# One list schedule for another: the same attention kernel with new tables of places

## The reference

```python
q = hidden_state @ Wq + bq                      # 512 x 1024
k = encoder_hidden_state @ Wk + bk              # 512 x 256
v = encoder_hidden_state @ Wv + bv              # 512 x 256
scores = einsum('bkgld,bksd->bkgls', q, k) / sqrt(32) + mask
attn = softmax(scores, axis=-1)
out = einsum('bkgls,bksd->bkgld', attn, v)
out = out @ Wo + bo
x = out + hidden_state
return (x - mean) * rsqrt(var + 1e-6) * gamma + beta
```

## Time and profile before

| | us |
|---|---|
| three timed runs | 1784.44, 1790.49, 1792.52 |
| their median | 1790.49 |
| profiled execution | 1783.61 |
| its span, first to last instruction | 1781.6 |
| mean granted TensorE clock | 0.967 |

### The profile page before, as it was taken

How to read it: one execution, slowest core, us unless ns; L and a number is a source line. 1 busy time by engine, 2 the same in 40 slices (tenths; PEclk the granted TensorE clock), 3 DMA queues, 4 the chain that set the end, 5 groups by cost and what they waited for, 6 DMA issues and landing times.

```text
span 1781.6 us, 38449 instructions
## 1 busy us (share of the span) xinstructions
PE 1638.9 (92%) x14048; PEld 1102.8 (62%) x14048; DVE 1469.6 (82%) x2773; ACT 1352.6 (76%) x3186; POOL 936.7 (53%) x731
## 2 busy tenths in 40 slices
PE   3898889899999989999899999999999998999895
PEld 2565556576667666677566666666665765657653
DVE  4589888789888897889889898888977988877875
ACT  3568777668887797877878789877987778786783
POOL 5426342426843476534845268444765348455381
PEclk8999999999999999999999999999999999999998
DMA  9659887747875578665896478856796647954321
GB/s 177 185 142 217 240 238 192 172 122 181 282 215 136 138 218 271 170 151 142 217 286 168 118 187 276 219 132 146 200 280 177 151 125 210 292 163 112 94 99 54
DMA packets 357291, 325.00 MB, mean 182 GB/s; under 512 B 145776, under 2 KB 248176, under 8 KB 357104
## 3 DMA queue, kind: packets, MB, share of 16 engines
q1 hardware_dynamic: 357104, 322.56, 67.9%
HBM read 244.85 MB, written 83.89 MB: 185 GB/s over the span
## 4 chain that ended last, share of the span: by engine, by line
PE 64%; DVE 19%; ACT 7%; issue 4%; SPq 4%; DMA 1%; POOL 0%; DVEq 0%; ACTq 0%
PE bank L1958 34%; PE bank L2041 15%; PE bank L2021 9%; DVE turned_p L1856 9%; DVE bank L1843 7%; ACT probs L1748 4%; PE bank L2056 2%; SPq L1516 2%; PE bank L1998 1%; PE bank L2081 1%; PE bank L2069 1%; DVE shift L1843 1%; SPq L1464 1%; ACT part L1731 1%; DVE x_t L1816 1%
## 5 line engine op out<-in xcount | busy, mean ns | idle before, releaser
L1748 ACT ACTIVATE probs<-bank,shift 128x512 f32<-128x512 f32 x1024 | 698.1, 692 | 191.8 <-DVE shift L1843 177.3
L1958 PE MATMUL bank<-ring_hi,w_sb 128*128 128x512 f32 x2368 | 795.2, 399 | 28.7 <-ACT part L1731 10.7
L1843 DVE CUSTOM_DVE_ANT_0 bank<-bank,mask_l 128x512 f32<-128x512 f32 x1024 | 677.9, 707 | 112.4 <-PE bank L2021 111.0
L1856 DVE STREAM_TRANSPOSE turned_p<-probs 128x2048 f32<-128x2048 f32 x256 | 587.9, 2301 | 130.2 <-PE bank L2041 122.3
L1642 POOL TENSOR_TENSOR w_sb<-w_raw,w_sb 128x512 fp32r<-128x512 f32 x320 | 411.8, 1295 | 385.3 <-ACT w_sb L1698 384.9
L1958 PEld LDWEIGHTS bank<-ring_hi,w_sb 128*128 128x128 f32 x2368 | 450.3, 190 | 146.6 <-ACT part L1731 21.4
L1958 PE MATMUL bank<-ring_lo,w_sb 128*128 128x512 f32 x1184 | 470.6, 397 | 0.0
L2021 PE MATMUL bank<-k_stack,q_stack 96*128 96x512 f32 x1024 | 409.9, 432 | 52.0 <-ACT probs L1748 44.9
L2041 PE MATMUL bank<-turned_p,v_all 32*32 32x512 f32 x8192 | 311.1, 643 | 25.3 <-DVE turned_p L1856 24.1
L2021 PEld LDWEIGHTS bank<-k_stack,q_stack 96*128 96x128 f32 x1024 | 187.3, 189 | 225.1 <-ACT probs L1748 134.5
L1654 POOL TENSOR_TENSOR ring_lo<-x_t,ring_hi 128x512 fp32r<-128x512 f32 x168 | 214.6, 1290 | 98.5 <-ACT ring_hi L1710 97.5
(11 more groups left out here) (75 smaller groups left out, 967.0 us busy)
## 6 DMA issues: line engine op xcount, KB each, us to landing
w_raw<-w_d SPq DMA_DIRECT2D x144, 256.0 KB, 4.1
q_stack<-q_hi_d SPq DMA_DIRECT2D x128, 256.0 KB, 4.6
w_raw<-in_L_xattn_Wo_dram SPq DMA_DIRECT2D x128, 256.0 KB, 3.2
q_hi_d<-part_hi SPq DMA_DIRECT2D x64, 256.0 KB, 3.4
q_lo_d<-part SPq DMA_DIRECT2D x64, 256.0 KB, 4.2
q_stack<-q_lo_d SPq DMA_DIRECT2D x64, 256.0 KB, 4.5
v_all<-v_d SPq DMA_DIRECT2D x256, 64.0 KB, 2.3
out_dram<-y_sb SPq DMA_DIRECT2D x32, 512.0 KB, 4.3
```

What stands on the lines that cost most here:

```text
L1748: nc.scalar.activation(probs[:, st % 2, h, :], S_ps[n % N_S][:, :], ACT.Exp, scale=-1.0, bias=shift[:, g % 2, i:i + 1], accum_out=sums[:, ...
L1843: nc.vector.tensor_tensor_reduce(out=S_ps[n % N_S][:, :], in0=S_ps[n % N_S][:, :], in1=mask_l[:, st, :], scale=-1.0, scalar=HIGHEST, op0=A ...
L1856: nc.vector.transpose(turned_p[:, :, :, st, :].rearrange("p j h c -> p h j c"), probs[:, st % 2, :, :].rearrange("p h (j c) -> p h j c", c ...
L1958: mm = nc.tensor.matmul(C[c][:, :], w_sb[:, n_w, (1, 0, 0)[third], d % 4, :], (hi, lo, hi)[third], start=(n == 0), stop=(n == 23))
```

## The change

Only the numbers in `BASE` and `PLACES` are changed, in all five kinds of batch. The list still has the same 8579 steps; their order differs. No function, wait, buffer or `WINDOWS` entry is touched. The diff is 1787 lines; its core, with `score`, `max` and `turn` of two groups and the places of `pv` in the steady kind of batch:

```diff
-BASE = {1: 255.61, 2: 463.14, 3: 669.69, 4: 876.25, 5: 1082.81, 6: 1289.37, 7: 1496.78}
+BASE = {1: 251.80, 2: 463.68, 3: 673.19, 4: 880.68, 5: 1088.16, 6: 1295.65, 7: 1503.13}
...
     "mid": {
         "score": (
-            (-0.99, -0.29, 1.34, 2.96, 3.66, 5.29, 5.98, 11.28, 11.52, 11.76, 15.4, 16.1, 17.73, 19.82, 20.11, 20.78),
-            (26.47, 26.7, 26.94, 32.24, 32.48, 32.71, 34.8, 37.06, 37.76, 38.46, 39.62, 40.78, 41.48, 42.1, 45.01,
-             45.71),
...
+            (-0.46, 0.24, 0.94, 2.1, 7.37, 7.6, 7.84, 11.93, 12.63, 13.33, 14.03, 14.73, 15.43, 18.53, 19.23, 19.93),
+            (21.56, 22.26, 22.96, 30.39, 30.63, 30.86, 32.95, 35.19, 35.43, 37.05, 37.75, 38.45, 39.65, 44.83, 45.53,
+             46.23),
...
         "max": (
-            (0, 0.64, 3.55, 4.19, 4.97, 5.74, 6.44, 13.73, 14.38, 15.02, 17.9, 18.54, 19.19, 20.45, 21.1, 21.74),
...
+            (0, 2.98, 3.67, 4.35, 9.89, 10.57, 11.26, 12.39, 13.09, 13.79, 16.77, 17.46, 18.14, 19.52, 20.2, 20.89),
...
         "turn": (
-            (11.5, 15.67, 22.39, 24.62),
-            (34.63, 40.82, 44.98, 50.06),
...
+            (7.59, 14.47, 21.57, 23.87),
+            (32.91, 38.19, 43.24, 49.15),
...
-        "pv": (27.64, 52.41, 81.48, 109.22, 131.26, 158.73, 185.69, 213.24),
...
+        "pv": (26.29, 51.57, 78.93, 106.79, 128.64, 156.83, 184.39, 210.75),
```

More of the change, by code:

```diff
@@ new lines @@
+            (160.31, 160.83, 162.04, 162.56),
+            (184.1, 184.62, 185.14, 186.35),
+            (213.01, 213.53, 214.05, 214.57),
+            (236.19, 236.71, 237.23, 237.75),
+            (259.91, 260.43, 260.95, 261.47),
+        ),
+        "stack": (50.64, 72.48, 82.39, 105.26, 127.71, 151.02, 176.26, 202.37),
+        "recip": (83.41, 107.66, 133.25, 157.61, 182.45, 209.26, 233.12, 256.84),
+        "spread": (83.73, 108.81, 133.73, 157.93, 182.77, 209.74, 234.45, 258.08),
+        "v_load": (59.65, 63.25, 86.57, 111.51, 135.14, 163.69, 186.09, 213.79),
@@ new lines @@
+            (167.08, 167.6, 168.81, 169.33),
+            (194.93, 195.45, 196.66, 197.18),
+            (220.91, 221.43, 221.95, 222.47),
+        ),
+        "stack": (-19.29, -1.39, 21.49, 45.24, 69.53, 98.23, 128.27, 154.45),
+        "recip": (28.78, 52.5, 75.77, 110.07, 137.45, 166.61, 192.16, 215.65),
+        "spread": (29.1, 52.97, 76.09, 110.97, 138.11, 167.86, 193.23, 216.55),
+        "v_load": (-14.83, 8.89, 32.63, 55.67, 90.8, 117.48, 139.58, 168.49),
+        "pv": (27.53, 50.57, 85.7, 112.38, 134.48, 162.67, 190.23, 216.59),
@@ L515 @@
-        "y_add o": (73.78, 79.49, 94.3, 100.35, 106.94, 121.41, 128.75, 144.66),
+            (41.73, 45.23),
+            (51.68, 55.48),
+            (63.86, 71.62),
+            (80.34, 81.65),
+            (85.64, 89.83),
+            (92.84, 98.35),
+            (109.68, 111.59),
+            (112.88, 115.21),
+        ),
+        "keep o": (72.13, 78.92, 85.92, 99.61, 106.19, 113.1, 126.91, 134.7),
+        "v_turn": (None, None, 165.88, 187.08),
+        "v_store": (None, None, 168.04, 188.81),
@@ L528 @@
+        "z_store o": (182.88, 191.65, 203.85, 212.39),
+        "root o": 160.37,
+        "rstd o": 166.81,
     },
@@ new lines @@
+            (161.24, 161.76, 162.97, 163.49),
+            (189.09, 189.61, 190.82, 191.34),
+            (215.07, 215.59, 216.11, 216.63),
+        ),
+        "stack": (-13.08, 3.39, 21.17, 47.68, 69.89, 96.37, 122.29, 148.15),
+        "recip": (28.23, 53.5, 78.05, 107.36, 131.86, 160.78, 186.33, 212.52),
+        "spread": (28.55, 53.96, 78.37, 108.26, 132.18, 162.02, 187.39, 212.84),
+        "v_load": (-17.99, 8.37, 31.39, 56.67, 84.03, 111.89, 133.74, 162.66),
+        "pv": (26.29, 51.57, 78.93, 106.79, 128.64, 156.83, 184.39, 210.75),
@@ L767 @@
-        "y_add o": (72.27, 77.81, 93.34, 99.39, 105.98, 120.44, 127.78, 143.69),
+            (46.71, 48),
+            (49.29, 54.58),
+            (55.87, 68.86),
+            (71.59, 74.2),
+            (79.6, 81.59),
+            (86.24, 97.11),
+            (98.55, 106.97),
+            (108.88, 110.17),
+        ),
+        "keep o": (64.91, 72.38, 79.48, 93.01, 99.3, 106.85, 120.94, 128.72),
+        "v_turn": (None, None, 160.05, 181.24),
+        "v_store": (None, None, 162.21, 182.97),
@@ L780 @@
+        "root o": 154.53,
+        "rstd o": 160.98,
     },
@@ new lines @@
+            (211.86, 212.98, 211.86, 212.51),
+        ),
+        "stack": (-12.08, 4.04, 21.68, 45.5, 69.64, 96.09, 124.52, 152.07),
+        "recip": (28.23, 52.95, 77.09, 107.67, 133.12, 160.24, 185.74, 207.42),
+        "spread": (28.55, 54.1, 78.88, 109.15, 133.44, 160.73, 186.36, 207.74),
+        "v_load": (-17.99, 9.44, 31.39, 56.8, 86.35, 113.74, 136.52, 163.4),
+        "pv": (26.29, 51.7, 81.25, 108.64, 131.42, 158.3, 184.49, 207.54),
+        "sel": (33.65, 59.75, 87.91, 115.3, 138.31, 166.82, 191.38, 213.89),
```

1040 lines of the change are left out of this document (492 added, 548 removed), and 396 rows, old and new, of the table PLACES.

## The result

The new order takes 1793.5 us (median of 20 runs, 1791.6 to 1796.7), the old one 1787.4 (20 runs, 1781.8 to 1792.7): a ratio of 1.0036 [1.0025, 1.0047], slower by a third of a per cent. That is less than the 0.5% that the prediction calls no change, but it is clear of 1 and on the other side of the forecast's sign. The profiled execution spans 1791.5 us where the old one spanned 1781.6: +9.9.

The account below looks back on a forecast made before the run. TensorE (92% busy) and VectorE (82%) were near their limit, with a circular ring of three score banks and the clock next. Inner batches -3, first and last -3, clock 0: 1790.5 - 6 = about 1784 us, range 1765 to 1806.

Parts of the forecast that it names:

- Counting work by section: TensorE and VectorE work between successive PV blocks of a steady batch: the new order adds 0.3 us a batch, no gain.
- What the order can gain: Section length beyond its work, 8.5 us a batch, shrinks as minimums and exponentials come earlier; -0.5 us a batch taken overall.
- The ring's waits: Circular waits among three score banks, exponentials, VectorE's minimums, probability transposes and PV blocks; 43 us of VectorE and ScalarE per batch.
- at the worst +1.2: Upper bound per inner batch: margins stay, and 0.3 us after PV is added in the three sections TensorE bounds.
- First and last batch: Batches 0 and 7: runs of scores move their ends, no term stands out; -3 us for both, bounds -8 and +6.
- Loads and helpers at nothing: GpSimd's and SyncE's steps, shifted by a few places, and the loads of queries and weights cost 0 us.
- The clock: Slow PV blocks after a starved TensorE: group 1 +4.4 us, group 6 -5.5; net about 0, bounds -11 and +14.
- Rival A: Order made for slower engines leaves usable slack, margins halve: -4.0 us per inner batch, about 1766 us; chance 0.22.
- Rival B: Slower through starved stretches before PV blocks: +4.4 at group 1, +8 new slow blocks, +4 kept margins; 1807 us; chance 0.25.
- Rival C: The ring sets the pace, so any sensible order with equal counts ends at 206 us a batch: 1790 us; chance 0.10.
- The signs set down beforehand: Right if full-clock inner batches take 204.5 to 206.5 us, with the named g7, g6 and slow-block values.
- the sign of being wrong: A full-clock batch over 207.5 us, read as the 0.3 us after a PV block not being hidden.

Follow-up runs that it names:

- keep_early: New order with ScalarE's copy of the fourth key-value tile moved earlier in the steady batches, from 172.89 to 169.75; 1788.1 us, ratio 0.9988 to the old order.
- base_even: New order with batches 3 to 7 placed 2.03 earlier, so the seam between batches 2 and 3 matches the following ones; 1789.3 us, ratio 1.0007 to the old order.
- mid_new: Old order with only the table of the steady batches (2 to 6) exchanged for the new one; 1806.7 us, ratio 1.0088 to the old order.
- mid_old: New order with only the table of the steady batches (2 to 6) exchanged for the old one; 1787.0 us, ratio 0.9986 to the old order.
- fill_before: Old order with six matmuls nobody reads before group 1's PV block and seven before group 6's, batches 2 to 6; 1772.1 us, ratio 0.9904 to the old order.

## Why the prediction was wrong

The forecast was 1784 us and the measurement 1793.5, inside the range; the sign was wrong. On the profiled execution -6 us were forecast, from -3 for the inner batches, -3 for the first and the last, and 0 for the clock. They came out at +18.5, -3.3 and -5.3, together +9.9. Point by point:

- **Counting work by section** (+0.3 a batch): held where it counted most. Group 7 was to grow by 1.9 us of VectorE's minimums and grew by 2.1 (20.8 to 22.9); group 6 was to lose 0.7 and lost 0.9; group 1 was to lose 0.5 and lost 1.0 at full clock (28.6 to 27.6). It failed in groups 2 and 3, forecast as 0.6 lighter: TensorE is busy for all of group 2's 28.02 us, so its two more scores counted (+0.4), not VectorE's lighter work.
- **"What the order can gain"** (-0.8 a batch): this is the step that failed. The margins between a section's work and its length, 8.5 us together, were to shrink; by the prediction's own counts of work they grew to about 10.8. They shrank in g1 and g6 alone (by 0.5 and 0.2). A steady batch came out at 208.6 us where 205.5 were forecast: 0.7 too little in g0, 1.1 in g2 and g3, 0.85 in g5, 0.4 in g7. The ring's waits did get shorter (42.9 to 39.1 us in batch 4), but the batch grew by 2.6 without its slow block: waits of the ring and length of a section are not the same thing. The bound "at the worst +1.2" was too low as well: it let margins stay and never grow. `keep_early` shows why they can: an order decides for each queue what stands ahead of the one copy that frees a bank, and the count of a section's work doesn't see it. For six inner batches the whole was to be -3 us; three of them (3 to 5) gave +2.5 to +3.3 each. What makes up the misses in g0, g3 and g7 was not tested.
- **A term was missing: the seams.** The working spoke of inner batches as if they were alike. Batch 2 has 5.4 us over a steady batch of its own order, all of it in its group 7 (28.6 against 22.9), and `base_even` took it away; batch 1 has +5.9 against the old order, of which 3.2 are in group 7 (20.8 to 24.0). Batch 6 gives 3.7 back, 4.4 of it in its group 7, ahead of the last kind of batch. Neither batch was tried by itself; that a seam can cost about 5 us and more was shown in `mid_new`, `mid_old` and `base_even`.
- **First and last batch** (-3): -2.7 net in batch 0 and -0.6 in batch 7, so -3.3. Right in size, though batch 0's slow blocks took 1.4 back.
- **Loads and helpers at nothing:** held. TensorE waited for no weight half in batch 4.
- **The clock** (0, bounds -11 and +14): slow blocks -5.3. Group 1 was slow in all five batches, as forecast, for the reason given. Those five cost 2.0 us each, and group 6 kept one slow block in batches 2 to 6 rather than half: with four projection matmuls before it the block was slow in one batch of five, and with one unread matmul in the old order in none. But the working took every slow block for the clock. By the estimate above 4.3 of the 26.7 us were holes at full clock, also in the block of the earlier trace rows, and the kernel after had none. The clock by itself moved by about -1 us, near the 0 of the forecast; the -4.3 have no term in it, and that this order had none of them may be luck. The gap in group 5, whose low clock is not in a PV block, wasn't foreseen; its price is in the 1.4 us of the `keep`.
- **Rival A** (packing pays) is refuted by the steady batches: net of slow blocks none is under 208.6. **Rival B** named the right side; of its price, the +4 for margins that stay was too small, and of the +8 for new slow blocks 1.5 came, one block in batch 0. **Rival C**, that any order with the same counts ends at 206, is refuted too.
- **The signs set down beforehand:** g7 near 22.5 and g6 under 27.5, slow blocks at g1 in five batches and fewer than four at g6: all came. A batch over 207.5 at full clock was the sign of being wrong. No inner batch of the kernel after ran at full clock throughout. Net of its slow block each is at 208.6 or more; with the early `keep`, which takes the low clock out of group 5, they are at 207.2. So the sign was met in part, and not for the reason written beside it: the score after a PV block still comes 4.39 us after it.

The Trainium skill (TensorE: Matmul & The Clock Gate, "The HAM clock gate") has the ramp penalty under 1% of a typical kernel's span. That sentence stands with the first matmuls of a kernel, so it is no rule on falls in the middle of one, as the prediction used it. Here those falls, in 12 blocks, cost an estimated 22 us of the 1781.6 (26.7 less 4.3), 1.3%.

The sign might have been called from the rows at hand: the one term that was counted (+0.3 a batch) pointed to slower, and the gain set against it had no row of its own.

## What to carry to other kernels

When only an order changes, count the work of each section and then look, for each buffer that is about to be reused, at what stands ahead of the instruction that frees it in its engine's queue; don't credit a gain to shorter waits in a ring that doesn't end the section. Cut the trace at the seams between differently ordered parts and forecast each seam by itself, for there a shift of 1% of a batch moved 5.6 us. Where a short burst of small matmuls follows a stretch of lone ones, try unread matmuls in the gaps before it. And look at the granted clock of a slow block before calling the clock its cause: some here were slow at full clock.

## What the runs showed of the hardware

- What TensorE did ahead of a PV block went with its granted clock: at group 1 of the new order it was low in 25 of 25 blocks without filling and in 1 of 10 with it. The clock moves between 1.00 and about half, 2.4 and 1.2 GHz. A matmul that nobody reads counts: in the old order the 20 filled blocks of groups 1 and 6 all ran at 1.00.
- A PV block can be slow at full clock: 12 blocks in twelve traces took 4.7 to 7.1 us at 1.00, each with a transfer of the instruction queue in it. The cause is likely but not shown.
- Unread matmuls were nearly free: with 13 of them in its gaps, the old order's batch 4 kept its 206.0 us (206.1 in `fill_before`).
- The spread of the runs went with the regularity of the slow blocks: 11 us over 20 runs before, 5 us after, where group 1 was slow in every steady batch of the profiled execution. That this is the cause is argued, not shown.
- A square root between exponentials cost ScalarE 2.9 us, two table loads of 1.28 us and 0.30 us of work. The same loads stand in every kernel here, and in batch 4 of the kernel after, where they lie around a PV block, TensorE did not wait for them.
